# An attention and expert kernel on TensorE: fewer identity products, one load on another queue, one down tile in another place

## What is computed

```python
xn = layernorm(x)
# attention, block by block
proj = xn @ W + b
w = exp(tanh((proj @ xn.T) * lw)) * (1 - eye)      # lw = 1/|i-j|, 0 on the diagonal
attn = (w / (w.sum(-1) + 1e-7)) @ xn
# experts: 8 of them, 2 chosen per row, hidden size 176
scores = sigmoid(xn @ gate_w.T); top 2 of scores + expert_bias
routed = sum over chosen e of (relu((score_e * xn) @ up_e.T) ** 2) @ down_e.T
shared = (relu(xn @ shared_up.T) ** 2) @ shared_down.T
out = x + attn + routed + shared
```

## Time and profile before

| | |
|---|---|
| Runs | 122.89, 121.48, 122.90 us; median 122.89 |
| The profiled execution | 122.78 us, span 120.9 us |
| Busy share of the span | PE 93%, PEld 70%, DVE 83%, ACT 76%, POOL 55% |
| Granted clock of PE | 1.00 over the span |
| DMA | 3.84 MB read and 2.10 MB written; 16 DMA engines |

### The profile page before, as it was taken

The page is one execution under the profiler, slowest core; times in us unless marked ns, Lnnn a source line. Parts: engine busy times, 40 slices in busy tenths (PEclk is TensorE's granted clock), DMA queues, the critical chain, the costliest instruction groups (busy, mean ns, idle before and its releaser), DMA issues.

```text
span 120.9 us, 2792 instructions
## 1 busy us (share of the span) xinstructions
PE 112.6 (93%) x916; PEld 84.5 (70%) x916; DVE 99.8 (83%) x316; ACT 92.1 (76%) x137; POOL 67.0 (55%) x117
## 2 busy tenths in 40 slices
PE   3977799999999999999999999999999999999591
PEld 3954446967678785879587767878587958768490
DVE  6957889898888989989888988898997698978621
ACT  1837879888889786979689768978697968996630
POOL 3129999922997389626981599338962405160000
PEclk9999999999999999999999999999999999999999
DMA  3999106959299929693938957782967493869962
GB/s 91 341 388 405 47 0 119 91 99 173 51 187 90 238 41 205 78 179 77 173 74 204 119 100 139 166 142 56 153 134 187 67 172 75 198 119 52 238 159 87
DMA packets 47821, 17.28 MB, mean 143 GB/s; under 512 B 44992, under 2 KB 45760, under 8 KB 47808
## 3 DMA queue, kind: packets, MB, share of 16 engines
q1 hardware_dynamic: 47232, 15.44, 65.6%
q10 hardware_dynamic: 576, 1.68, 3.9%
HBM read 3.84 MB, written 2.10 MB: 49 GB/s over the span
## 4 chain that ended last, share of the span: by engine, by line
PE 79%; DMA 8%; ACT 8%; issue 2%; POOL 1%; DVE 1%; POOLq 0%; ACTq 0%
PE out_ps L857 14%; PE h_ps L826 13%; PE dots L781 9%; PE side L802 9%; DMA hiddenT<-hidden 8%; PE out_ps L845 5%; PE side L815 5%; PE out_ps L886 4%; PE small L771 4%; PE small L753 4%; PE out_ps L839 4%; ACT hidden L434 3%; PE small L741 3%; ACT upT L353 1%; PE small L762 1%
## 5 line engine op out<-in xcount | busy, mean ns | idle before, releaser
L601 DVE SCALAR_TENSOR_TENSOR gated<-h_ps,gates 128x1408 bf16<-128x1408 f32 x31 | 50.0, 1613 | 5.2 <-PE h_ps L826 5.1
L434 ACT ACTIVATE hidden<-gated 128x1408 bf16<-128x1408 bf16 x31 | 42.6, 1378 | 2.2 <-DVE gated L601 2.0
L857 PEld LDWEIGHTS out_ps<-downT,hiddenT 128*128 128x128 bf16 x341 | 21.5, 98 | 7.8 <-issue 5.2
L857 PE MATMUL out_ps<-downT,hiddenT 128*128 128x128 bf16 x341 | 24.1, 219 | 1.5 <-DMA hiddenT<-hidden 1.5
L826 PE MATMUL h_ps<-upT,xnTb 128*128 128x512 bf16 (+1 forms) x96 | 24.4, 363 | 0.2
L251 POOL TENSOR_SCALAR xn<-x_sb,meanvar,rstd 128x128 f32<-128x128 f32 x28 | 21.9, 795 | 0.7
L276 POOL TENSOR_SCALAR_AFFINE_SELECT probs<-probs 128x256 f32<-128x256 f32 x16 | 6.5, 409 | 22.6 <-ACT probs L400 22.6
L781 PE MATMUL dots<-projT,xnT 128*128 128x256 f32 x60 | 15.9, 388 | 0.6 <-ACT projT L391 0.6
L802 PEld LDWEIGHTS side<-xn,probs 128*128 128x128 f32 x120 | 15.0, 191 | 1.4 <-issue 0.5
L802 PE MATMUL side<-xn,probs 128*128 128x129 f32 x120 | 15.9, 275 | 0.0
L826 PEld LDWEIGHTS h_ps<-upT,xnTb 128*128 128x128 bf16 x96 | 8.1, 97 | 7.9 <-DVE gated L601 1.8
(11 more groups left out here) (96 smaller groups left out, 163.2 us busy)
## 6 DMA issues: line engine op xcount, KB each, us to landing
x_sb<-in_x SPq DMA_DIRECT2D x7, 256.0 KB, 8.5
out_y<-final SPq DMA_DIRECT2D x7, 256.0 KB, 2.3
up_raw<-in_up ACTq DMA_DIRECT2D x1, 704.0 KB, 6.8
down_raw<-in_down ACTq DMA_DIRECT2D x1, 704.0 KB, 8.6
hiddenT<-hidden SPq DMA_TRANSPOSE x31, 3.7
out_y<-final SPq DMA_DIRECT2D x2, 128.0 KB, 1.7
late_sb<-in_late SPq DMA_DIRECT2D x1, 192.0 KB, 8.8
x_sb<-in_x ACTq DMA_DIRECT2D x1, 128.0 KB, 2.6
```

The lines of the kernel that those rows point to most:

```text
L434: a.activation(hidden[:, t, :], gated[:, t, :], ACT.Square).then_inc(squared, 1)
L601: v.scalar_tensor_tensor(out=gated[:, t, :].rearrange("p (e h) -> p e h", e=E), in0=h_ps[:, 0:NH].rearrange("p (e h) -> p e h", e=E), scal ...
L857: last = t_.matmul(out_at(t), hiddenT[:, c % 2, t, j, :], downT[:, j, :], start=(t == 0 and j == 0), stop=(t >= 2 and j == KT - 1), skip_g ...
```

## The change

The warm-up has eight products instead of twelve. The load of the down weights is issued on SP's queue, behind late and ahead of chunk 3's x, and no longer on ACT's queue. In the step k = 2 of PE's loop, down_tile(0, 1) stands behind rest(2) and shared_down_rest(0) instead of ahead of them.

```diff
--- before.py
+++ after.py
@@ -141,7 +141,7 @@
         sup_made, sup_taken, sup_squared = sem("sup_made"), sem("sup_taken"), sem("sup_squared")
         out_made, sdown_made, final_ready, stored = sem("out_made"), sem("sdown_made"), sem("final_ready"), sem("stored")
 
-        WARM = 12
+        WARM = 8
         HALF = NH // 2
         PARTS = ((0, 4), (4, 8), (8, KT))
         K = 2
@@ -207,6 +207,7 @@
             load_x(1)
             load_x(2)
             sp.dma_start(late_sb[:, :], late).then_inc(late_loaded, 16)
+            sp.dma_start(down_raw[:, :, :].rearrange("p k d -> p (k d)"), down).then_inc(down_loaded, 16)
             for c in range(3, NCH):
                 load_x(c)
             for k in range(1, NCH):
@@ -346,7 +347,6 @@
             act.dma_start(x_sb[:, 0, 2:4, :].rearrange("p t d -> p (t d)"), x[0, :, 2 * D:4 * D]).then_inc(x_first[1], 16)
             act.dma_start(early_sb[:, :], early).then_inc(early_loaded, 16)
             act.dma_start(up_raw[:, :], up).then_inc(up_loaded, 16)
-            act.dma_start(down_raw[:, :, :].rearrange("p k d -> p (k d)"), down).then_inc(down_loaded, 16)
 
             def cast_up():
                 act.wait_ge(up_loaded, 16)
@@ -912,10 +912,10 @@
                 f, c, o = k, k - 1, k - 2
                 up_tile(c, 0)
                 attend(c, 0)
+                rest(f)
+                shared_down_rest(o)
                 if k == 2:
                     down_tile(0, 1)
-                rest(f)
-                shared_down_rest(o)
                 up_tile(c, 1)
                 shared_down_main(o)
                 down_tile(o, 2)
```

## The result

Twenty runs of each kernel: the changed one has a median of 122.00 us (121.31 to 123.48), the old one 122.65 (121.48 to 124.40, and one run at 193.26). The ratio is 0.9949, 95% interval 0.9927 to 0.9972: half a per cent faster, inside the forecast range and 0.1 us from the forecast. The ratio leaves out runs over 1.5% above the fastest, some of which are part of what this change does, so medians and counts here are of all runs. Seven of the twenty runs of the changed kernel lie between 123.2 and 123.5 and none between 122.5 and 123.2, which no median tells.

What follows compares the result with a forecast made beforehand. PE was taken to set the pace from the loop's start to the tail, so gain could come only from reaching it earlier. 122.78 less 0.77 (warm-up) and 0.16 (moved tile), load 0, gave 121.85, forecast 121.9 us; range 121.0 to 123.7.

Steps and rivals of the forecast that it cites:

- Eight products, 0.77 us: Kernel head: with four fewer warm-up products, the first transposed x is copied 0.77 us earlier, then limited by xn.
- my cap of 0.82: Kernel head: chunk 2's x, waited for until 8.81, lets at most 0.82 us of gain through to the first weigh.
- The moved tile, 0.16 us: Second down tile in step 2: other products hide its transposing DMA, saving PE's 0.16 us wait; bounds 0 to 0.3.
- My upper bound of 0.3: Moved tile: a gain of at most 0.3 us, twice the wait, if the DMA would else land later against PE.
- The load, 0: Down weights on SP's queue: worth 0, landing near 10.8 us, hidden ahead of GpSimd's cast.
- Rival 1: Head: the clock stays low through rest and project of chunk 0; 123.6 us (0.14), or 125.2 and more (0.06); chance 0.20.
- Rival 2: Head gives nothing because chunk 2's x or the up weights land later; only 0.16 is left, 122.6 us; chance 0.13.
- Rival 3: Warm-up: the old kernel's lowest run, 121.48, had an earlier clock rise; the kernel after takes 121.3 us; chance 0.15.
- Its second part: Of the rival on an earlier clock rise: the kernel after always gets there, 121.3 us (121.48 less 0.16).
- the seven signs: Profile after: warm-up end 5.4, copy 7.0, weigh 11.6, no cast wait, no moved-tile wait, no PE hole behind, span 120.0.
- The absence of a hole behind the tile: Profile after: PE runs without a hole behind the moved down tile of step 2.
- the span: Profile after: the whole execution's span near 120.0 us, against 120.9 before.

Runs made afterwards that it cites:

- warm_undone: The changed kernel with twelve warm-up products again, load and order as changed: median 121.87 us, ratio 0.9960 to the kernel before.
- load_undone: The changed kernel with the down weights back on ACT's queue: median 121.96 us, ratio 0.9971 to the kernel before.
- after_look: The changed kernel, unaltered, run and profiled once more: a single run of 123.23 us.
- order_alone: The kernel before with only the second down tile of step 2 moved: median 121.81 us, ratio 0.9954 to the kernel before.
- order_undone: The changed kernel with the second down tile put back ahead of the rest products: median 122.48 us, ratio 1.0019 to the kernel before.
- warm_alone: The kernel before with only the warm-up cut from twelve to eight products: median 122.79 us, ratio 0.9998 to the kernel before.
- warm16: The changed kernel with sixteen warm-up products instead of eight: median 123.44 us, ratio 1.0040 to the kernel before.
- after_again: The changed kernel, unaltered, measured and profiled a second time: median 121.93 us, ratio 0.9958 to the kernel before.
- fill2: The changed kernel with two more identity products between chunk 0's transposes and rest(0): median 121.75 us, ratio 0.9931 to the kernel before.
- after_third: The changed kernel, unaltered, measured again beside three variants on the same chip: median 121.95 us, ratio 0.9980 to the kernel before.
- warm4: The changed kernel with four warm-up products instead of eight: median 123.41 us, ratio 1.0075 to the kernel before.

## Why the prediction was right, and where it was right for the wrong reason

The time was 0.1 us off, and that is luck: the two main terms are wrong in opposite directions, and the start of the sum is off too. The gain was forecast as 0.93 from 122.78; by the medians of twenty runs it is 0.65 from 122.65.

- **Eight products, 0.77 us.** The mechanism was right where the profile had it: xn and not PE became the limit, and the copy came at 6.79 to 7.25 in the profiles with eight products. DVE's wait for x ended at 8.54 and not at 8.81, so my cap of 0.82 did not hold either, and 0.87 came through. What failed is the step that took one execution's place of the rise for the program's. Where the level rises early, twelve products end at 6.3 and xn is the limit anyway: the gain is 0 (7.04 against 7.04, warm_undone and load_undone). Between the profiles of before, whose rise I had put near 6.9, and after it is 0.87. Where it rises later, eight products lose: after_look's first dots come at 11.84, order_alone's, with a copy as late as 8.16, at 11.45. Over all runs the sum is about 0 at the median (121.93 to 122.00 with eight, 121.81 and 121.87 with twelve, in the new order), and in the mean the kernel after is 0.4 worse (122.36 over 45 runs against 121.99 over 24).
- **The moved tile, 0.16 us.** Right in kind, but it measured three to five times as much. By the medians it is 0.5 (order_undone less after), 0.75 (before less order_alone) and 0.8 (warm_alone less load_undone, where the load and the number of products are the same); by the pairs of profiles 0.67 and 0.35. Two steps failed. I took the wait from one execution, with a DMA of 4.67 where the other profiles with a read on that tile have 4.8 to 5.0 (but for warm16's 3.9), and I put the reordering itself at nothing, where the pairs show 0.2 beside the wait. My upper bound of 0.3 came from doubling the wait, with no look at how the DMA's 4.67 came about.
- **The load, 0.** Right, as far as the runs can tell. Down weights landed 7.9 after an issue at 2.7, at 10.6 (I had 10.8); the late weights at 8.9 instead of 11.0; the up weights as before.
- **Rival 1, 123.6 with a chance of 0.20.** Its mechanism stands in after_look's profile, at 123.23. Twelve of 45 runs of the changed kernel lie at 123.2 to 123.5 with a mean granted clock of 1.00 as after_look has, 1.2 to 1.5 over their group's median; that they are all of this kind is likely, and shown for the one that has a profile. I had added 1.72 for it, the whole of rest and project once more; in after_look they take 1.4 more than in after_again, and the first dots come 1.3 later. I had it as a way the median could go; it is a share of the runs. The Trainium skill (TensorE: Matmul & The Clock Gate, Part 1: The HAM clock gate) says that the throttled level is the default and that activity releases it. fill2's profile and the counts with four, eight and ten products agree. The same section warns that the recorded clock events are not to be trusted in full. The 1.00 beside records of 648 and 1142 ns agrees.
- **Rival 2** (x lands later) did not occur: the wait for it ended at 8.54 (8.92 at the latest in the other profiles, in order_undone, whose head is as early as load_undone's). **Rival 3** asked for an earlier rise with twelve products. warm_undone shows that there is such a rise (copy at 7.04); whether the old kernel's lowest run had it stays open, for that run has no trace. Its second part, that the kernel after gets there always, is wrong.

What a profile of the changed kernel would show: five of the seven signs held. The absence of a hole behind the tile did not, by the late DMA of the third tile in that execution, and the span did not (120.8 for 120.0); after_again and after_third, without the hole, have spans of 120.3 and 120.0.

## What to carry to other kernels

When a stretch before a wait runs at a clock level that changes by itself, one profile says what happened in one run; look at more than one, and at the spread of all runs, before pricing an edit there. Warm-up work can be put where the engine waits anyway and not only ahead of the first useful work: eight products and two in a gap of 0.78 us were as fast as twelve at the front, as far as twelve runs can tell. And if one wait of a tuned kernel ends at a DMA whose like lands a microsecond sooner elsewhere, move independent work in front of it: the move was worth three to five times the 0.16 us that one profile put on it. An order that is changed can also change what the joints cost (0.2 here), so read the start of a later piece in both kernels and not the wait alone.

## What I had not expected of the hardware

**A transposing DMA under way when a block of instructions is read lands later.** Over the fourteen profiles of this study, at the second and third tile of chunk 0:

| | landed after us | cases |
|---|---|---|
| no 16 KB read while under way | 3.5 to 3.7 | 14 |
| read while under way, in eleven profiles | 4.7 to 5.1 | 11 |
| read while under way, in after_look, warm4 and warm16 | 3.9 to 4.0 | 3 |

The source views of the issuing line for the second tile's DMA, after (no read) and after_again (read):

```profile
L195 SPq DMA_TRANSPOSE hiddenT<-hidden x1: 1393/1393/1393, 20.6 to 20.6; - x1
...
DMA to landing us min/median/max: 3.5/3.5/3.5
```

```profile
L195 SPq DMA_TRANSPOSE hiddenT<-hidden x1: 1382/1382/1382, 20.9 to 20.9; - x1
...
DMA to landing us min/median/max: 5.0/5.0/5.0
```

The read begins between 22.7 and 23.8 us in eleven profiles and between 26.1 and 27.9 in three; two of these three are those in which the level stayed low. The two lower rows of the table differ in when it begins: 1.9 to 2.7 us after the DMA's issue in the second row, and 0.3 to 0.6 us after it in after_look, warm4 and warm16. What sets its place I don't know, and no run here moved it on purpose; the link is a coincidence seen fourteen times in fourteen, not an effect that was switched on and off. Nor is it the only case of a late landing. Later in the kernel before, the DMAs issued at 36.0 and 108.4 took 4.7 and 4.9 us with a 16 KB read under way (from 37.8 and 109.4), but the one issued at 83.0 took 4.7 with another transposing DMA 1.5 us behind it and only one smaller read, of 0.01 MB, on another instruction queue.

**The clock can also fall at the end.** In the profile of warm_alone the last transposing DMA keeps PE idle for 1.55 us, and behind it the granted clock drops, this time in the record as well (stretches of 3 us; PEclk is the third number from the end of the line):

```profile
110.00:113.00 3.00, 1.40 (x17) 0.92 (x17) 2.93 (x8) 2.02 (x2) 0.00 (x0) 1.00 1.25 141
113.00:116.00 3.00, 3.00 (x29) 2.71 (x27) 0.06 (x1) 0.88 (x2) 0.00 (x0) 0.75 0.94 233
116.00:119.00 3.00, 3.00 (x41) 3.00 (x39) 0.76 (x2) 1.08 (x2) 0.00 (x0) 0.68 0.00 0
```

PE's timeline there, and that of the kernel after, with an idle time of 1.47 and no drop:

```profile
114.19 1.83 PE L845 MATMUL out_ps<-late_sb,shidden 128*128 128x128 f32 x8
...
115.82 1.38 PE L857 MATMUL out_ps<-downT,hiddenT 128*128 128x128 bf16 x11
```

```profile
114.56 1.16 PE L845 MATMUL out_ps<-late_sb,shidden 128*128 128x128 f32 x8
...
115.55 0.78 PE L857 MATMUL out_ps<-downT,hiddenT 128*128 128x128 bf16 x11
```

In the chain of waits the three groups of tail products that follow take 0.67, 0.56 and 0.40 us more than in the kernel after: the last addition is at 119.48 instead of 118.21. The mean granted clock of that execution is 0.986. A mean of 0.97 to 0.99 stands in up to three runs of a group of twelve: in 11 of the 93 runs with eight products (fill2 among them) and in 2 of the 12 with sixteen, but in none of the 36 with ten or twelve in the new order and in 1 of the 99 of the kernel before that ran beside the experiments. Such runs took 122.7 to 124.9 us. The idle time alone doesn't decide it: load_undone's profile has 1.62 us of it at the same place, and PEclk stays at 1.00. What decides between the two tails, and what the warm-up has to do with the end of the kernel, no run here shows.
